# State-space mixer: norms kept compact, states with time outermost, one matmul for four heads' state products, a second projection tile between states and scores, scan ahead of the recurrence

## The reference

```
proj  = x @ W_in.T ;  value = silu(causal_conv(proj_value)) ;  gate, dt, kd, A from proj and parameters
bc    = value @ W_bc.T, four vectors of 32 per head and token: Bz, Bx, Cz, Cx
bc    = bc / (norm(bc) + eps)
per token:  S = 1 / (1 + dt*kd + dt^2*A)
            z = S * (z - dt*A*s + dt*Bz*u) ;  s = s + dt*z + dt*Bx*u
            y = Cz . z + Cx . s
out   = ((y + skip*value) * silu(gate)) @ W_out.T
```

## Time and profile before

| | |
|---|---|
| median of three runs | 2338.43 us |
| profiled execution: time, span | 2331.21 us, 2329.6 us |
| busy over the span | DVE 88%, PE 81%, ACT 47%, POOL 4% |
| granted TensorE clock, mean | 0.913 |
| 500 us to 1000 us of the span: DVE, PE, ACT busy | 474.91, 426.65, 237.42 us |

### The profile page before, as it was taken

One profiled execution on the slowest core, in us unless ns is written; L12 is line 12 of the kernel. 1 busy time (PEld: TensorE's weight loads), 2 busy tenths in 40 slices (PEclk: granted clock), 3 DMA queues, 4 the chain that ended last, 5 costly groups with the idle time before them and its releaser, 6 DMA issues. The chain is left out here.

```text
span 2329.6 us, 78341 instructions
## 1 busy us (share of the span) xinstructions
PE 1875.7 (81%) x31266; PEld 1078.5 (46%) x31266; DVE 2050.5 (88%) x5467; ACT 1083.9 (47%) x1700; POOL 84.5 (4%) x28
## 2 busy tenths in 40 slices
PE   6777468987888898888888889887888898367886
PEld 3333134444444444444444444444444444246775
DVE  6887599999999999999989989998999998487774
ACT  4665235454444454445544444544545455034553
POOL 0000000000000000000000000000000000153300
PEclk9898779999999999999999999999999999578997
DMA  4555634655555565545655554665455543433400
GB/s 139 178 214 184 178 92 112 147 134 131 124 127 125 119 150 130 125 106 134 145 123 126 138 124 109 145 143 125 110 126 129 117 113 87 159 154 136 145 27 27
DMA packets 224663, 300.25 MB, mean 129 GB/s; under 512 B 96784, under 2 KB 114192, under 8 KB 218128
## 3 DMA queue, kind: packets, MB, share of 16 engines
q1 hardware_dynamic: 174416, 212.11, 35.9%
q10 hardware_dynamic: 48704, 78.68, 13.3%
q0 software_dynamic: 1152, 4.19, 0.5%
HBM read 240.85 MB, written 50.86 MB: 125 GB/s over the span
## 5 line engine op out<-in xcount | busy, mean ns | idle before, releaser
L670 PE MATMUL m_ps_a<-m_valT,m_w_bc 128*128 128x512 f32 x2048 | 962.1, 619 | 59.8 <-DMA m_valT<-scratch_valT 32.0
L670 PEld LDWEIGHTS m_ps_a<-m_valT,m_w_bc 128*128 128x128 f32 x2048 | 389.8, 198 | 491.1 <-issue 483.7
L958 DVE TENSOR_TENSOR m_prod<-m_psi,m_shear 128x128 f32<-128x128 f32 x960 | 369.0, 384 | 0.0
L962 DVE TENSOR_TENSOR m_psi<-m_psi,m_prod 128x128 f32<-128x128 f32 x960 | 368.4, 384 | 0.0
L818 ACT ACTIVATE m_sq<-m_ps_a 128x512 f32<-128x512 f32 x256 | 152.8, 597 | 372.4 <-PE m_ps_a L670 367.9
L833 ACT ACTIVATE m_kT<-m_ps_g 128x512 f32<-128x512 f32 x128 | 72.0, 596 | 249.8 <-PE m_ps_g L716 249.8
L716 PE MATMUL m_ps_g<-m_ident,m_k 128*128 128x128 f32 x512 | 88.9, 330 | 103.8 <-DVE m_k L1060 103.5
L695 PE MATMUL m_ps_g<-m_q,m_k 32*64 32x64 f32 x8192 | 122.8, 232 | 45.3 <-issue 38.9
L695 PEld LDWEIGHTS m_ps_g<-m_q,m_k 32*64 32x64 f32 x8192 | 107.5, 133 | 100.2 <-ACT m_dX L840 53.3
L819 ACT ACTIVATE m_raw<-m_ps_a 128x512 f32<-128x512 f32 x256 | 151.6, 592 | 0.0
L755 PEld LDWEIGHTS m_ps_y<-m_q,m_X 32*16 32x16 f32 x7168 | 105.2, 94 | 84.1 <-issue 84.1
(11 more groups left out here) (143 smaller groups left out, 3061.7 us busy)
## 6 DMA issues: line engine op xcount, KB each, us to landing
m_scale<-scratch_norm SPq DMA_DIRECT2D x256, 256.0 KB, 5.3
m_w_bc<-in_w_bcT ACTq DMA_DIRECT2D x252, 256.0 KB, 4.7
m_shear<-scratch_n_alpha SPq DMA_DIRECT2D x64, 256.0 KB, 5.3
m_shear<-scratch_beta SPq DMA_DIRECT2D x256, 64.0 KB, 4.1
m_det<-scratch_gd SPq DMA_DIRECT2D x256, 64.0 KB, 4.5
scratch_gateT<-gate SPq DMA_DIRECT2D x8, 1024.0 KB, 3.9
scratch_valT<-val SPq DMA_DIRECT2D x8, 1024.0 KB, 4.5
scratch_svgT<-svg SPq DMA_DIRECT2D x8, 1024.0 KB, 5.5
```

Source lines behind the costliest of these rows:

```text
L670: mm = pe.matmul(ps_a[j % 2].ap(), w_bc[:, j, kt, :], valT[:, kt, :], start=(kt == 0), stop=(kt == KI - 1), skip_group_check=True)
L958: dve.tensor_tensor(prod.ap(), psi_t[half][:, :, :, :, t], shear_t[half][:, :, :, t].unsqueeze(1).to_broadcast([P, 2, 2, HALF * NC]), ALU. ...
L962: ins = dve.tensor_tensor(psi_t[half][:, :, :, :, t + 1], psi_t[half][:, :, :, :, t], prod[:, :, ::-1, :], ALU.add)
```

## The change

1. Compact norms. `sum_squares` multiplies with a matrix `seg_sum` that puts head and token segment on the output rows, 32 matmuls of 64 columns in place of 4 of 512, so that the result is compact already. The root works on 128x64 in place of 128x512, the four DMAs per group and their wait go, and DVE's three instructions on the norms move in between those that form q.
2. Time outermost. `psi` and the step factors `shear` are laid out so that a step's 128 elements are contiguous. ACT lays the factors out (`lay_shear`, two ACTIVATEs per group in place of one, through a staging tile that SP loads) and gathers one group's `psi` back to time innermost (`gather_psi`, 128x2080, one per group), which k and q read. The shares of the steps are 36, 36, 36, 20 in place of 32 each.
3. State products. One matmul with 128 columns of weights and 64 moving columns gives all four heads (and the products across heads, which are not used): 16 matmuls, for all 8 chunks, in place of 56 for 7. `copy_dX` picks the blocks on the diagonal, four ACTIVATEs of 32x256 in place of two on 128 partitions.
4. PE's order: all of tile 0 ahead of the state products, and tile 1 between them and the scores.
5. The scan `log_sum(b, group + 1)` stands ahead of the chain over chunks, not at the group's end.

```diff
@@ sum_squares
-                    for j in range(NJ):
-                        mm = pe.matmul(ps_s[j * N:(j + 1) * N, :], head_sum.ap(), sq[:, j, :],
+                    for seg in range(SEGS):
+                        for j in range(NJ):
+                            mm = pe.matmul(ps_s[j * N:(j + 1) * N, 0:SEG], seg_sum[:, seg, :],
+                                           sq[:, j, seg * SEG:(seg + 1) * SEG],
...
@@ chunk_states
                     for part in range(2):
-                        for h in range(HP):
-                            heads = slice(c // 2 * P + h * N, c // 2 * P + (h + 1) * N)
-                            mm = pe.matmul(ps_dX(c)[h * N:(h + 1) * N, part, :], kT[rows_of(c), part, heads],
-                                           u[rows_of(c), s, c // 2, h * DH:(h + 1) * DH], start=True, stop=True,
...
+                        mm = pe.matmul(ps_dX(c, part), kT[rows_of(c), part, c // 2 * P:(c // 2 + 1) * P],
+                                       u[rows_of(c), s, c // 2, :], start=True, stop=True, skip_group_check=True)
@@ inner
-                        product(b, group + 2, 0, (0, 1, 2))
+                        product(b, group + 2, 0, range(KI))
...
-                    for c in range(NC - 1):
+                    for c in range(NC):
                         chunk_states(s, c)
                     if ahead:
-                        product(b, group + 2, 0, (3,))
+                        product(b, group + 2, 1, range(KI))
                     pe.wait_ge(dX_ready.sem, dX_ready.at(b, group))
                     pe.wait_ge(q_ready.sem, q_ready.at(b, group))
                     for c in range(NC):
                         scores(s, c)
                     if ahead:
-                        product(b, group + 2, 1, range(KI))
                         product(b, group + 2, 2, range(KI))
@@ copy_dX
-                    for odd in range(2):
-                        count = NC // 2 - odd
-                        ins = act.activation(dX[:, odd:NC - 1:2].rearrange("p c r d -> p c (r d)"),
...
+                    for h in range(HP):
+                        rows, cols = slice(h * N, (h + 1) * N), slice(h * DH, (h + 1) * DH)
+                        ins = act.activation(dX[rows].rearrange("p (k i) r d -> p k (i r) d", k=HP),
...
@@ ACT: new
+                def lay_shear(b, group, src, loads=None):
...
+                    act.activation(dst[0], chunks(src[:, 0, :]), ACT.Copy, scale=A[:, group:group + 1])
+                    act.activation(dst[1], chunks(src[:, 1, :]), ACT.Copy).then_inc(shear_ready.sem, shear_ready.step)
+                def gather_psi(b, group):
...
+                    act.activation(psi_g.ap().rearrange("p r k c t -> p (r k) c t"),
+                                   psi[:, half, :, :, :, cols].rearrange("p t r k c -> p (r k) c t"),
+                                   ACT.Copy).then_inc(psi_ready.sem, psi_ready.step)
@@ SP spread_scales
-                    sp.wait_ge(scaled.sem, scaled.at(b, group - 1))
+                    sp.wait_ge(q_ready.sem, q_ready.at(b, group - 1))
@@ DVE body
-                            scales(b, group + 1, advance)
+                            log_sum(b, group + 1)
                         dve.wait_ge(y_made.sem, y_made.at(b, group - 1))
                         dve.wait_ge(dX_ready.sem, dX_ready.at(b, group))
...
-                        if not (last and group == LAST):
-                            log_sum(b, group + 1)
                         advance(end_at - done)
```

More of the change, by code:

```diff
@@ L471, in mix, with place, ps_dX @@
         ps_y = ps("y")
-        def ps_dX(c):
-            col = PAIRS * C + c // 2 * 2 * DH
-            return ps_g[:, 2 + c % 2, col:col + 2 * DH].rearrange("p (r d) -> p r d", r=2)
+        def place(c):
+            return (c // 4 * 2 + c % 2) * 2 + c // 2 % 2
+        def ps_dX(c, part):
+            bank, col = place(c) // 2, PAIRS * C + (place(c) % 2 * 2 + part) * HP * DH
+            return ps_g[:, bank, col:col + HP * DH]
         consts_in = sem("consts_in")
@@ L825, in norms @@
                     act.wait_ge(sums_made.sem, sums_made.at(b, group))
-                    act.wait_ge(compact_in.sem, compact_in.at(b, group * NJ - 1))
-                    act.activation(rows_.ap(), ps_s.ap(), ACT.Sqrt).then_inc(norm_ready.sem, norm_ready.step)
+                    act.wait_ge(rows_stored.sem, rows_stored.at(b, group - 1))
+                    act.activation(compact.ap(), ps_s[:, 0:SEG], ACT.Sqrt).then_inc(norm_ready.sem, norm_ready.step)
                 def copy_kT(b, group):
@@ L867, in _ @@
                 for group in range(HALF):
-                    scale_beta(0, group)
+                    lay_shear(0, group, first_stage[group], HALF)
+                act.wait_ge(shear_ready.sem, shear_ready.at(0, HALF - 1))
                 for j in range(NJ):
@@ L872, in _ @@
                 for group in range(HALF, HG):
-                    scale_beta(0, group)
+                    lay_shear(0, group, stage)
                 det_log(0, 0)
                 det_inverse(0, 0)
+                gather_psi(0, 0)
                 for j in range(NJ):
@@ L885, in _ @@
                 det_inverse(0, 1)
+                gather_psi(0, 1)
                 def body(b, last):
@@ L895, in body @@
                             norms(b, group + 2)
+                        if not last and group == 0:
+                            lay_shear(b + 1, 0, stage)
                         if here:
@@ L904, in body @@
                             det_log(b, group + 2)
-                        if not last and group == 0:
-                            scale_beta(b + 1, 0)
-                        if not last and group < LAST:
-                            scale_beta(b + 1, group + 1)
                         if ahead:
                             evacuate(b, group + 3, 1, not (last and group == LAST - 3))
+                        if more:
+                            gather_psi(b, group + 2)
+                        if ahead:
                             evacuate(b, group + 3, 2, not (last and group == LAST - 3))
+                        if not last and group < LAST:
+                            lay_shear(b + 1, group + 1, stage)
                         if more:
@@ L931, in _ @@
                     for comp in range(2):
-                        dve.memset(psi[:, row, comp, :, :, 0:1], 1.0 if row == comp else 0.0).then_inc(own.sem, own.one())
+                        dve.memset(psi[:, :, 0, row, comp, :], 1.0 if row == comp else 0.0).then_inc(own.sem, own.one())
                 dve.wait_ge(own.sem, own.n)
@@ L1010, in _ @@
                     if t == C // 2:
-                        scales(0, 0, lambda n: None)
+                        apply_factors(0, 0, invert_norms(add_eps(0, 0)))
                     step_rows(0, 0, t)
@@ L1019, in body @@
                         r4 = raw[s]
+                        here = not (last and group == LAST)
                         psi_b, half, slot = (b, 1, group) if group < HALF else (b + 1, 0, group - HALF)
-                        done, end_at = 2 * slot * STEPS, 2 * (slot + 1) * STEPS
+                        done, end_at = SHARES[slot], SHARES[slot + 1]
                         if last and half == 0:
@@ L1075, in body @@
                         advance(1)
+                        if here:
+                            apply_factors(b, group + 1, inverted)
                         dve.tensor_tensor(q[s][:, 1, :], q[s][:, 1, :], kt[:, 0, :], ALU.subtract).then_inc(q_ready.sem, q_ready.step)
@@ L1097, in body @@
                             if c:
-                                dve.tensor_tensor(V.ap(), dX[:, c], X[:, c - 1], ALU.add).then_inc(own.sem, own.one())
+                                dve.tensor_tensor(V.ap(), dX[:, place(c)], X[:, c - 1], ALU.add).then_inc(own.sem, own.one())
                                 v_made = own.n
```

178 lines of the change are left out of this document (88 added, 90 removed).

## The result

The changed kernel takes 2619.53 us (median of 4 runs, 2612.35 to 2629.2), the kernel before, beside it, 2337.0 us: ratio 1.1212, 95% interval 1.1171 to 1.1253. It is 282.5 us slower; 2680 (2520 to 2850) was forecast. The profiled execution took 2629.2 us, with a span of 2627.5.

What follows compares the result with a forecast made beforehand. DVE, 95% busy, bounds the kernel. Distances of 32.4 (45), 30.0 (15), 28.4 (twice) and 23.5 us, plus 34 for loop ends, make 2022 against 1677.5: +345 on 2331.2, -3, +7: 2680 us (2520 to 2850).

Steps and rivals of the forecast that it cites:

- the step that decides: DVE's scan, ahead of the chain, waits for ACT's logarithms behind copy and tile 0; DVE idles about 9 us per group.
- early logarithms: Rival: logarithms on ACT come before the copy, so only the late copy delays the chain; 2403 us, chance 0.09.
- DVE stays the bound: Rival: copy and logarithms come in time, DVE sets the pace; 24 us per group put, 2209 us, chance 0.04.
- lasting low clock: Rival: PE, idle in every group, stays at the lower clock through the state products; 3045 us, chance 0.06.
- K to the state products: From the end of DVE's last instruction on k (K), through PE's transposes and tile 0: 4.5 plus 1.9 us for clock.
- state products: PE's 16 matmuls, 32 loads of 128 columns, 0.11 us per pair: 3.5 us against 1.03; bounds 1.03 and 5.6.
- copies: ACT's four copies of 256 elements of the state products: 1.2 us by interpolation, bounds 0.42 and 2.0.
- chain starts at: DVE's first chain instruction, 15.6 us after its last instruction on k ends; in the kernel before 6.9 us.
- chain to next K, 36 steps: DVE from the chain's start to the end of the next group's k, in groups with 36 steps: 16.75 us.
- Groups with 20 steps: DVE needs 6.7 plus 7.65 us from chain to the next k's end; 15 such distances of 30.0 us.
- The clock: PE, waiting for k in nearly every group, slows between k and the state products: 1.9 us lost, bounds 0 and 2.95.
- Steps: DVE's steps on contiguous elements take 283 ns instead of 384, starts 0.20 us apart instead of 0.30: 3.2 us per group.

Runs made afterwards that it cites:

- Runs 1 and 2: First: changed kernel with the scan back behind the masks, 2383.26 us. Second: kernel before with only the scan moved ahead of the chain, 2557.89 us.
- run 3: Changed kernel with the next group's logarithms right behind its norms on ACT, scan still ahead of the chain: 2345.42 us, ratio 1.0035.
- run 7: Changed kernel with gather_psi done twice, 3.84 us more on ACT in each group: 2649.85 us, ratio 1.1316.
- run 12: Changed kernel with logarithms behind the norms, two of tile 0's four parts behind the state products, lay_shear ahead of gather_psi: 2265.93 us, ratio 0.9693.
- run 11: Changed kernel with the state products one matmul per head and two copies, as before: 2494.66 us, ratio 1.066.
- run 4: Changed kernel with the logarithms right behind the norms, plus the old state products and two copies: 2369.13 us, ratio 1.0109.

## Why the prediction was right, and where it was off

The mechanism, the step that decides and the sign were right: the scan, put ahead of the chain, waits for logarithms that stand behind the copy of its own group's state products. Runs 1 and 2 show it from both sides (236 us back, 221 lost), run 3 shows that it is the order on ACT, not the scan as such. The rivals "early logarithms" (2403 us), "DVE stays the bound" (2209) and "lasting low clock" (3045) did not come.

Its terms, in us per group (mean of 63):

| term | forecast | measured |
|---|---|---|
| K to the state products | 6.4 | 6.26 |
| state products | 3.5 | 2.05 |
| copies | 1.2 | 1.5 |
| tile 0 out, table, Ln | 3.2 | 3.25 |
| scan | 1.13 | 1.15 |
| chain starts at | K + 15.6 | K + 14.35 |
| chain to next K, 36 steps | 16.75 | 16.7 to 17.2 |
| the same, 20 steps | 14.35 | 16.5 to 16.9 |

- **State products**: the mis-sized term. I took 0.11 us for each load and matmul; 32 pairs take 2.05 us, 0.064 each, hardly above the 0.056 of the stream., whose loads stand behind longer matmuls, gave no floor for a load. 1.45 us in 62 groups are 90 us too much. The rule of the Trainium skill cited there (TensorE: Matmul & The Clock Gate, Part 3) would have given 5.6 us, by the estimate made there from rows; this trace does not bear it out, although the pairs of one chunk share their row groups.
- **Copies**: interpolated too low; 32x256 takes 375 ns, four 1.5 us: 20 us the other way.
- **Groups with 20 steps**: two microseconds too short, for two reasons. Behind a row's fourth group a new half of the states begins, and its first step waits 2.2 us for `lay_shear` in seven rows, which I had counted as hidden: from the masks to K 9.94 us there, where I had 7.65. Behind the eighth group that wait is 0.2 us or none but in one row; there the loop's end, which I counted apart at 4.9 us, costs some 2.3: 9.97 us from the masks to K. The two errors cancel by luck: these 15 groups took 480 us, and 450 with 34 for the loop's ends were forecast.
- **The clock**: the sum came out right (6.26 us to the state products), in part by luck. In 24 of 64 groups PE comes to the transposes late, mostly 1 to 1.5 us behind k, 0.5 us in the mean, which I had left out; from there to the state products it takes 5.7 us, where the forecast had 4.5 at the full clock, so the clock costs some 1.2 us and not 1.9. PE idles 5.6 us per group (31.24 x 0.18), near the 5 forecast, but for k only 1.3 (82.3/63), the rest for masks, squares and "issue". In the group shown 2.34 us of "issue" stand ahead of the slow stretch.
- **Steps**: 288 ns, as forecast (283). DVE works 22.7 us per group (31.24 x 0.728), 25.3 before. The gain is there, but DVE was no longer the bound, so it became idle time.
- **`gather_psi`**: 3.84 us, the second of my two values, and hidden, as run 7 shows.
- **Start and end**: span less the distances is 659.5 us, 652.1 before: +7, where I had -3.

For the profiled execution 2673 us were forecast, and 2629 came: the distances took 54 us less (1968 for 2022), start and end 10 more. The median lies 10 us below that execution, where I had added 7; that makes the 60 us by which the forecast was high.

The change was worth something, with its order mended: run 12 keeps every edit but where two parts of tile 0, the logarithms and `lay_shear` stand, and is 3.1% faster than the kernel before.

## What to carry to other kernels

When an instruction is moved forward on an in-order engine, look on the producer's engine for what stands ahead of its input: if that input is queued behind something that depends on the same group, the move closes a loop, and every piece of the loop then counts at full length (run 11: 125 us), though the same pieces count for nothing or with the other sign when the loop is open (run 4). Here work saved on the busiest engine was worth nothing until the loop through the other engines was as short; an order that was harmless (`lay_shear` last) then became a wait.

## What the runs showed of the hardware that I had not expected

Loads of 64x128 weights between matmuls of 64 columns cost next to nothing: 0.064 us a pair, while a load by itself lasts 189 ns (groups by form, the changed kernel):
```profile
L693 PEld LDWEIGHTS m_ps_g<-m_u,m_kT 64*128 64x128 f32 x2048 | 124.0, 189 | 49.2 <-issue 49.2
```
ACT pays for distance in SBUF: 2080 elements read 512 bytes apart take 3.84 us, 1.85 ns each, and 512 elements written apart (`lay_shear`) 1.19 and 1.11 us, where the kernel before scales 512 contiguous ones in place in 0.71 us.

PE stops in mid-line with no releaser, 30 times for 1.1 to 3.3 us in `mix` of the changed kernel, the loop's ends apart. The stretch behind the one shown ran at a granted clock of 0.58 (1012.74 to 1020.00 us), against 1.00 from 1023.90 to 1036.00. As in run 4, the distances between these stops are multiples of 256 instructions of PE's queue, to within 5. Each of the 30 ends 1.2 to 1.6 us after a 16 KiB packet has landed on the DMA queue that the profile names `instruction` (queue, kind: packets, MB, share of 16 engines):
```profile
q8 instruction: 243, 3.98, 0.7%
```
So do the 29 of run 3; the 68 of run 4, which has 278 such packets, end 1.2 to 1.9 us after one. PE has some 60,700 instructions, 237 times 256, so this looks like PE waiting for its own code; no run changed it to prove that.
